# One pending tile's down projection placed behind the next tile's gate and up products, its transposes in another PSUM tensor

## The chip, the cores and the metric

The kernel runs on all 8 cores of one Trainium2 chip. Every core runs the same program on its own 2,048 tokens; the cores do not talk to each other. The metric is the device time of the slowest core, in microseconds (us).

## What is computed

One transformer layer on x of 4 x 4096 x 2048, in float32 outside the products: a retention-like attention block and a feed-forward block whose hidden values are made 2:4 sparse. The part that matters here is the second one:

```
x = x + layernorm(attn(layernorm(x)))
h = silu(xn @ w_gate) * (xn @ w_up)            # xn = layernorm(x); 2048 -> 8192
h = h where |h| is among the 2 largest of its group of 4, else 0
x = x + layernorm(h @ w_down)                  # 8192 -> 2048
```

## The kernel before

**Before the feed-forward block.** A core first runs the attention block over its 16 tiles of 128 tokens, up to about 2,480 us of the profile. It leaves the normalized and transposed tiles in DRAM (`s_xn3T`) and the residual in `s_x2`. Nothing of this is touched.

**The feed-forward block, `ffn()`** (lines 638 to 789). The 8192 hidden columns are cut into NIC = 8 blocks `ic` of ICW = 1024. For each block the loop runs over the 16 tiles `t`. One iteration does this:

- SP loads the tile from `s_xn3T` into `bpool[t % 2]` (L718).
- PE makes gate and up: 64 matmuls of 128x512 into `psA` (L729, L732), gate in the first 1024 columns of `psA`, up in the others.
- ACT takes Silu of gate (L740); DVE multiplies it with up (L746) into one of three buffers of h (the trace names them t_mat, l_mat and fp; in the last block only the first two are used, since `fpool[2]` is needed elsewhere).
- ACT writes |h| (L751); seven small DVE operations find the second largest of each group of four (L761 to L777), one compares (L781), and one masks h (L784). This is called the mask chain below.

**The drain.** `drain(...)` makes the down projection of one tile whose h is ready: PE transposes h (8 float32 transposes, L675), ACT copies them back as bf16 (L680), PE runs 32 matmuls of 128x512 into `psB` (L689), DVE copies `psB` out (L697), and POOL adds the result to `s_acc` in DRAM by an accumulating DMA (L704; L700 in the first block). A list `pending` holds the tiles whose drain is still to come. It holds up to two tiles in blocks 0 to 6 and one in block 7.

**The end of a block.** While tile 15 is in gate and up, `load_q` loads and casts the next block's gate and up weights (32 half rows, DMAs on SP, casts on ACT at L617 and DVE at L613). Then the tiles still pending are drained back to back, and `load_fdc` loads the down weights of the next block.

**The last block.** There each drain is followed by `emit_ln4`: SP reads the sum back from `s_acc` (L646), DVE and ACT compute the layer norm (L310, L313, L315, L318, L652), DVE adds the residual (L656), and SP stores the tile of y (L660).

**Order.** Each engine runs its own list of operations in the order in which `P.op` was called, SP's DMAs too. Before an operation, its engine waits for the semaphores of what it reads and overwrites, and nothing behind it starts until it has. `r_A[0]` and `r_A[1]` stand for the two halves of `psA`, `r_B[0]` and `r_B[1]` for those of `psB`. Below, d(t) is the drain of tile t and g(t) its gate and up matmuls.

Of the kernel before, what the change touches and what calls it, by code (L numbers as in the profile page):

```python
# [18 lines left out]
ICW = 1024  # L19
NIC = I // ICW  # L20
# [121 lines left out]
def build():  # L142
# [56 lines left out]
    psA = psm("psA", [128, D], F32)  # L199
    psB = psm("psB", [128, D], F32)  # L200
# [12 lines left out]
    P = Prog()  # L213
# [15 lines left out]
    r_ident = Res()  # L229
    r_vst = Res()  # L230
    r_carry = Res()
    r_A = [Res(), Res()]
    r_B = [Res(), Res()]
# [404 lines left out]
    def ffn():  # L638
# [6 lines left out]
        def emit_ln4(t):  # L645
            P.op("sync", lambda s, t=t: s.dma_start(out=fpool[2][:], in_=s_acc[t]),  # L646
                 dma=True, reads=[r_sacc[t]], writes=[r_fp[2]])
            mvp, rsp, rs = ln_stats(fpool[2][:], r_fp[2], par=t % 2)
            fx = t % 2
            P.op("sync", lambda s, t=t, fx=fx: s.dma_start(out=fpool[fx][:], in_=s_x2[t]),  # L650
                 dma=True, reads=[r_sx2[t]], writes=[r_fp[fx]])
            P.op("vector", lambda v, fx=fx, mvp=mvp, rsp=rsp: v.tensor_scalar(  # L652
                fpool[2][:], fpool[2][:], mvp[:, 0:1], rsp[:],
                ALU.subtract, ALU.mult),
                 reads=[rs], writes=[r_fp[2]])
            P.op("vector", lambda v, fx=fx: v.tensor_tensor(fpool[2][:], fpool[2][:],  # L656
                                                            fpool[fx][:], ALU.add),
                 reads=[r_fp[fx]], writes=[r_fp[2], r_fp[fx]])
            yres = Res()
            tok = P.op("sync", lambda s, t=t: s.dma_start(  # L660
                out=y_d[t * 128:(t + 1) * 128, :], in_=fpool[2][:]),
                dma=True, reads=[r_fp[2]], writes=[yres])
            out_toks.append(tok)

        def drain(pend):
            pt, pic = pend
            par = ((pic * NT + pt) % 3) if pic < NIC - 1 else (pt % 2)
            hsp = hbuf[par]
            hflat = hflats[par]
            rh = r_h[par]  # L670

            def trf(tt, hsp=hsp):
                ins = None
                for j in range(8):
                    ins = tt.transpose(psA[:, j * 128:(j + 1) * 128],  # L675
                                       hsp[:, j * 128:(j + 1) * 128], ident[:])
                return ins
            P.op("tensor", trf, reads=[rh, r_ident], writes=[r_A[0]])
            hT_flat = hflat
            P.op("scalar", lambda s, hT_flat=hT_flat: s.copy(hT_flat[:, 0:ICW],  # L680
                                                             psA[:, 0:ICW]),
                 reads=[r_A[0]], writes=[rh, r_A[0]])
            hT = hT_flat[:, 0:ICW].rearrange("p (a b) -> p a b", b=128)
            for q in range(4):
                def f(tt, q=q, hT=hT):
                    ins = None
                    for kc in range(q * 2, (q + 1) * 2):
                        for n in range(4):
                            ins = tt.matmul(psB[:, n * 512:(n + 1) * 512], hT[:, kc, :],  # L689
                                            fdc[:, kc, n * 512:(n + 1) * 512],  # L690
                                            start=(kc == 0), stop=(kc == ICW // 128 - 1))
                    return ins
                P.op("tensor", f, reads=[rh, r_fdc[q]], writes=[r_B[0], r_B[1]])
            dk = drr[0] % 4
            drr[0] += 1
            ev = stgF[dk]
            P.op("vector", lambda v, ev=ev: v.tensor_copy(ev[:], psB[:]),  # L697
                 reads=[r_B[0], r_B[1]], writes=[r_stgF[dk], r_B[0], r_B[1]])
            if pic == 0:
                P.op("gpsimd", lambda g, pt=pt, ev=ev: g.dma_start(  # L700
                    out=s_acc[pt], in_=ev[:]),
                    dma=True, reads=[r_stgF[dk]], writes=[r_sacc[pt]])
            else:
                P.op("gpsimd", lambda g, pt=pt, ev=ev: g.dma_start(  # L704
                    out=s_acc[pt], in_=ev[:], accum_op=ALU.add),
                    dma=True, reads=[r_stgF[dk]], writes=[r_sacc[pt]])
            if pic == NIC - 1:
                emit_ln4(pt)

        pending = []  # L710
        for ic in range(NIC):
            while pending:
                drain(pending.pop(0))
            load_fdc(ic)
            for t in range(NT):
# [2 lines left out]
                P.op("sync", lambda s, t=t, bx=bx: s.dma_start(out=bpool[bx][:],  # L718
                                                               in_=s_xn3T[t]),
                     dma=True, reads=[r_sxn3T[t]], writes=[r_bp[bx]])  # L720
                if len(pending) >= (2 if ic < NIC - 1 else 1):
                    drain(pending.pop(0))
                xT = bpool[bx][:].rearrange("p (a b) -> p a b", b=128)
                for q in range(4):
                    def f(tt, xT=xT, q=q):
                        ins = None
                        for kc in range(q * 4, (q + 1) * 4):
# [9 lines left out]
                         writes=[r_A[0], r_A[1]])  # L737
                    if t == NT - 1 and ic + 1 < NIC:
# [3 lines left out]
                     reads=[r_A[0]], writes=[r_fp[fx], r_A[0]])  # L742
# [6 lines left out]
                     reads=[r_A[1], r_fp[fx]], writes=[rht, r_A[1], r_fp[fx]])  # L749
# [3 lines left out]
                     reads=[rht], writes=[r_bp[2]])  # L753
# [9 lines left out]
                     reads=[r_bp[2]], writes=[r_bp[3]])  # L763
                P.op("vector", lambda v: v.tensor_tensor(mx1, a4[:, :, 0:1], a4[:, :, 1:2],  # L764
                                                         ALU.max),
                     reads=[r_bp[2]], writes=[r_bp[3]])
                P.op("vector", lambda v: v.tensor_tensor(mn2, a4[:, :, 2:3], a4[:, :, 3:4],
                                                         ALU.min),
                     reads=[r_bp[2]], writes=[r_bp[3]])
                P.op("vector", lambda v: v.tensor_tensor(mx2, a4[:, :, 2:3], a4[:, :, 3:4],  # L770
                                                         ALU.max),
                     reads=[r_bp[2]], writes=[r_bp[3]])
                P.op("vector", lambda v: v.tensor_tensor(mn1, mn1, mn2, ALU.max),
                     reads=[r_bp[3]], writes=[r_bp[3]])
                P.op("vector", lambda v: v.tensor_tensor(mx1, mx1, mx2, ALU.min),
                     reads=[r_bp[3]], writes=[r_bp[3]])
                P.op("vector", lambda v: v.tensor_tensor(mn1, mn1, mx1, ALU.min),  # L777
                     reads=[r_bp[3]], writes=[r_bp[3]])
# [4 lines left out]
                    reads=[r_bp[2]], writes=[r_bp[3]])  # L783
                P.op("vector", lambda v, cmpm=cmpm, hsl=hsl: v.tensor_tensor(  # L784
                    hsl[:, 0:ICW], hsl[:, 0:ICW], cmpm, ALU.mult),
                     reads=[r_bp[3]], writes=[rht])
                pending.append((t, ic))
        while pending:
            drain(pending.pop(0))
# [13 lines left out]
    handoff([r_fdc[0], r_fdc[1], r_fdc[2], r_fdc[3]] + r_stgF, r_wB)  # L803
    handoff([r_p0b[0], r_p0b[1]], [r_decay])
    ffn()
    P.barrier_wait("sync", out_toks)

# [49 lines left out]
```

How the kernel before makes its waits and increments, by code:

```python
            def body(h, ops=ops):  # L116
                for waits, fn, sname, n in ops:
                    for s, v in waits:
                        h.wait_ge(sems[s], v)
                    if fn is not None:
                        ins = fn(h)
                        if sname is not None:
                            ins.then_inc(sems[sname], n)
```

## Time and profile before

| | us |
|---|---|
| median of two runs | 6968.84 (6835.03 and 7102.64) |
| the profiled execution, its own time | 6868.66 |
| its span (slowest core, core 5) | 6867.1 |
| spans of the eight cores | 6807.3 to 6867.1 |
| PE busy in matmuls | 4399.4 (64%) |
| DVE busy | 2059.3 (30%) |
| ACT busy | 1007.7 (15%) |

The span runs from the first to the last instruction of a core. PE is TensorE, DVE is VectorE, ACT is ScalarE, POOL is GpSimd; SPq is the queue that issues most DMAs. Busy time of PE is made up of overlapping matmuls, so a 128x512 matmul shows as 0.38 us although one starts every 0.22 us. "PEclk" is the clock granted to TensorE as a share of 2.4 GHz. The feed-forward block takes about 4,380 of the 6,867 us: seven blocks of some 520 us and a last one of about 760.

### The profile page before, as it was taken

To read this page: it belongs to the slowest core of one execution; us is meant where nothing else is said; L and a number is where in the kernel's file an instruction comes from. 1 tells how busy PE (TensorE), PEld (TensorE's weight loads), DVE (VectorE), ACT (ScalarE), POOL (GpSimd) and SP (SyncE) were. 2 spreads that over 40 slices of the span, in tenths; PEclk is the share of its full clock that TensorE was granted. 3 is DMA by queue.
4 is the path that set the end of the run, shared out by engine and by line. 5 is a ranking of instruction groups with operands and counts; after the bars stand their busy time and mean duration, and the time that the engine had idled before them with its cause. 6 is when DMAs were issued, how large, how long until landed. Compare 5 with 4: busy or idle time off the path is not lost.

```text
span 6867.1 us, 51810 instructions; the slowest of 8 cores (6807.3 to 6867.1 us)
## 1 busy us (share of the span) xinstructions
PE 4399.4 (64%) x19374; PEld 2041.2 (30%) x19374; DVE 2059.3 (30%) x2796; ACT 1007.7 (15%) x1035; POOL 165.7 (2%) x232
## 2 busy tenths in 40 slices
PE   0236888547616668858758758858858848835554
PEld 0013444224303323323323323323323323312222
DVE  1523233212214433323223223322322323322333
ACT  2301111111111011111111111111111111111111
POOL 0000000000000000000000000000000000000000
PEclk9998778778858889979979979979979979967777
DMA  5400100132263331242352352352352352353333
GB/s 156 137 13 22 37 31 34 48 114 75 89 202 118 121 107 59 93 143 59 94 142 59 94 142 59 85 148 59 84 149 62 78 155 57 75 175 97 99 108 104
DMA packets 140830, 649.31 MB, mean 95 GB/s; under 512 B 15652, under 2 KB 15652, under 8 KB 107812
## 3 DMA queue, kind: packets, MB, share of 16 engines
q1 hardware_dynamic: 110630, 461.44, 20.6%
q0 software_dynamic: 29952, 184.56, 12.1%
q8 instruction: 156, 2.56, 0.2%
q14 instruction: 92, 0.75, 0.0%
HBM read 453.00 MB, written 192.94 MB: 94 GB/s over the span
## 4 chain that ended last, share of the span: by engine, by line
PE 57%; DMA 19%; DVE 10%; ACT 7%; issue 5%; SPq 1%; DVEq 0%; ACTq 0%; POOL 0%; POOLq 0%
PE psB L689 16%; PE psA L729 11%; PE psA L732 11%; PE psB L356 9%; PE psA L356 5%; DMA stg<-w_gate 3%; DMA stg<-w_down 2%; PE psA L336 2%; DMA stg<-w_up 2%; DMA s_acc<-wslotB 2%; ACT bp L751 2%; ACT fp L740 2%; DVE stats L310 1%; DMA stg<-Wg 1%; DMA stg<-Wo 1%
## 5 line engine op out<-in xcount | busy, mean ns | idle before, releaser
L729 PE MATMUL psA<-wslotA,bp 128*128 128x512 bf16 x4096 | 1566.8, 383 | 284.6 <-DMA bp<-s_xn3T 263.5
L732 PE MATMUL psA<-wslotA,bp 128*128 128x512 bf16 x4096 | 1565.8, 382 | 0.0
L729 PEld LDWEIGHTS psA<-wslotA,bp 128*128 128x128 bf16 x4096 | 403.6, 99 | 782.4 <-issue 307.9
L732 PEld LDWEIGHTS psA<-wslotA,bp 128*128 128x128 bf16 x4096 | 403.4, 98 | 490.0 <-issue 14.9
L356 PE MATMUL psB<-wslotA,bp 128*128 128x512 bf16 x2048 | 492.4, 406 | 44.2 <-ACT bp L341 44.2
L356 PE MATMUL psA<-wslotB,bp 128*128 128x512 bf16 x1536 | 373.3, 409 | 207.6 <-DMA bp<-s_ygT 207.6
L697 DVE COPY wslotB<-psB 128x2048 f32<-128x2048 f32 x128 | 293.3, 2291 | 673.4 <-PE psB L689 673.4
L740 ACT ACTIVATE fp<-psA 128x1024 f32<-128x1024 f32 x128 | 131.0, 1024 | 2310.9 <-PE psA L732 2310.8
L689 PE MATMUL psB<-wslotB,t_mat 128*128 128x512 bf16 x1472 | 397.0, 437 | 96.9 <-DVE bp L764 74.5
L689 PE MATMUL psB<-wslotB,l_mat 128*128 128x512 bf16 x1440 | 393.6, 441 | 95.0 <-DVE bp L764 76.6
L689 PE MATMUL psB<-wslotB,fp 128*128 128x512 bf16 x1184 | 319.3, 437 | 84.0 <-DVE bp L764 73.6
L336 PE MATMUL psA<-ident,fp 128*128 128x128 f32 x768 | 144.5, 368 | 267.0 <-DVE fp L519 216.5
L356 PEld LDWEIGHTS psB<-wslotA,bp 128*128 128x128 bf16 x2048 | 208.9, 103 | 322.0 <-issue 147.9
L356 PEld LDWEIGHTS psA<-wslotB,bp 128*128 128x128 bf16 x1536 | 158.6, 104 | 417.8 <-issue 298.7
L613 DVE CAST wslotA<-stg 128x1024 bf16<-128x1024 f32 x160 | 111.0, 694 | 547.6 <-DMA stg<-w_up 349.1
L689 PEld LDWEIGHTS psB<-wslotB,t_mat 128*128 128x128 bf16 x1472 | 157.9, 109 | 325.9 <-issue 205.6
L689 PEld LDWEIGHTS psB<-wslotB,l_mat 128*128 128x128 bf16 x1440 | 155.4, 110 | 323.3 <-issue 207.8
L617 ACT CAST wslotA<-stg 128x1024 bf16<-128x1024 f32 x160 | 167.0, 1044 | 560.6 <-DMA stg<-w_gate 312.9
L675 PE MATMUL psA<-ident,l_mat 128*128 128x128 f32 x360 | 56.6, 309 | 297.3 <-DVE l_mat L784 159.4
L675 PE MATMUL psA<-ident,t_mat 128*128 128x128 f32 x368 | 57.6, 308 | 284.0 <-DVE t_mat L784 146.6
L310 DVE BATCH_NORM_STATS2 stats<-fp 128x6 f32<-128x512 f32 x256 | 158.0, 679 | 234.3 <-DMA fp<-s_acc 224.6
L336 PEld LDWEIGHTS psA<-ident,fp 128*128 128x128 f32 x768 | 133.1, 197 | 282.8 <-issue 279.8
(128 smaller groups left out, 3250.0 us busy)
## 6 DMA issues: line engine op xcount, KB each, us to landing
s_acc<-wslotB POOLq DMA_DIRECT2D x128, 1024.0 KB, 7.7
stg<-w_gate SPq DMA_DIRECT2D x128, 512.0 KB, 5.6
stg<-w_up SPq DMA_DIRECT2D x128, 512.0 KB, 5.9
stg<-w_down SPq DMA_DIRECT2D x128, 512.0 KB, 6.1
bp<-s_xn3T SPq DMA_DIRECT2D x128, 512.0 KB, 3.3
fp<-x SPq DMA_DIRECT2D x48, 1024.0 KB, 5.2
stg<-Wq SPq DMA_DIRECT2D x32, 512.0 KB, 4.8
stg<-Wv SPq DMA_DIRECT2D x32, 512.0 KB, 4.5
```

Of the source, the lines that this page charges most:

```text
L310: ins = v.bn_stats(st6[:, 6 * i:6 * i + 6], src_ap[:, 512 * i:512 * (i + 1)])
L336: ins = t.transpose(psA[:, half * 1024 + j * 128:half * 1024 + (j + 1) * 128], src_ap[:, kc * 128:(kc + 1) * 128], ident[:])
L356: ins = t.matmul(psum[:, n * 512:(n + 1) * 512], xT_ap[:, kc, :], w_sb[:, kc, n * 512:(n + 1) * 512], start=(kc == 0), stop=(kc == KC - 1))
L613: P.op("vector", lambda v, dst_ap=dst_ap, k=k: v.tensor_copy(dst_ap, wstg4[k]), reads=[r_wstg4[k]], writes=[dst_res, r_wstg4[k]])
L617: P.op("scalar", lambda s, dst_ap=dst_ap, k=k: s.copy(dst_ap, wstg4[k]), reads=[r_wstg4[k]], writes=[dst_res, r_wstg4[k]])
L675: ins = tt.transpose(psA[:, j * 128:(j + 1) * 128], hsp[:, j * 128:(j + 1) * 128], ident[:])
L689: ins = tt.matmul(psB[:, n * 512:(n + 1) * 512], hT[:, kc, :], fdc[:, kc, n * 512:(n + 1) * 512], start=(kc == 0), stop=(kc == ICW // 128 ...
L697: P.op("vector", lambda v, ev=ev: v.tensor_copy(ev[:], psB[:]), reads=[r_B[0], r_B[1]], writes=[r_stgF[dk], r_B[0], r_B[1]])
L729: ins = tt.matmul(psA[:, n * 512:(n + 1) * 512], xT[:, kc, :], fgc[:, kc, n * 512:(n + 1) * 512], start=(kc == 0), stop=(kc == KC - 1))
L732: ins = tt.matmul(psA[:, 1024 + n * 512:1024 + (n + 1) * 512], xT[:, kc, :], fuc[:, kc, n * 512:(n + 1) * 512], start=(kc == 0), stop=(kc ...
L740: P.op("scalar", lambda s, fx=fx: s.activation(fpool[fx][:, 0:ICW], psA[:, 0:ICW], AF.Silu), reads=[r_A[0]], writes=[r_fp[fx], r_A[0]])
L751: P.op("scalar", lambda s, hsl=hsl: s.activation(habs[:, 0:ICW], hsl[:, 0:ICW], AF.Abs), reads=[rht], writes=[r_bp[2]])
```

## The change

Two things change in `ffn()`, and no amount of work changes. The transposes of h go to `psB` instead of `psA`, and the ACT copy reads them from there. The call of `drain` inside the tile loop moves from ahead of the gate and up matmuls of tile t to behind the mask chain of tile t; the number of tiles that may be pending stays two, or one in the last block.

```diff
@@ drain
-                    ins = tt.transpose(psA[:, j * 128:(j + 1) * 128],
+                    ins = tt.transpose(psB[:, j * 128:(j + 1) * 128],
                                        hsp[:, j * 128:(j + 1) * 128], ident[:])
-            P.op("tensor", trf, reads=[rh, r_ident], writes=[r_A[0]])
+            P.op("tensor", trf, reads=[rh, r_ident], writes=[r_B[0]])
             P.op("scalar", lambda s, hT_flat=hT_flat: s.copy(hT_flat[:, 0:ICW],
-                                                             psA[:, 0:ICW]),
-                 reads=[r_A[0]], writes=[rh, r_A[0]])
+                                                             psB[:, 0:ICW]),
+                 reads=[r_B[0]], writes=[rh, r_B[0]])
@@ tile loop of ffn
                 P.op("sync", lambda s, t=t, bx=bx: s.dma_start(out=bpool[bx][:],
                                                                in_=s_xn3T[t]),
                      dma=True, reads=[r_sxn3T[t]], writes=[r_bp[bx]])
-                if len(pending) >= (2 if ic < NIC - 1 else 1):
-                    drain(pending.pop(0))
                 xT = bpool[bx][:].rearrange("p (a b) -> p a b", b=128)
...
                      reads=[r_bp[3]], writes=[rht])
+                maxp = 2 if ic < NIC - 1 else 1
+                if len(pending) >= maxp:
+                    drain(pending.pop(0))
                 pending.append((t, ic))
```

## Rows read from the trace of the kernel before

**Rows 1.** Timeline of one tile in block 2: start us, us, engine, line, idle before.

```profile
3714.53 1.02 ACT L740 ACTIVATE fp<-psA 128x1024 f32<-128x1024 f32 x1 [22.84 <-PE psA L732]
3715.73 1.22 DVE L746 TENSOR_TENSOR t_mat<-psA,fp 128x1024 f32<-128x1024 f32 x1 [12.64 <-ACT fp L740]
3715.81 1.06 PE L675 MATMUL psA<-ident,fp 128*128 128x128 f32 x8 [1.38 <-ACT fp L740]
3717.05 1.06 ACT L751 ACTIVATE bp<-t_mat 128x1024 bf16<-128x1024 f32 x1 [1.49 <-DVE t_mat L746]
3718.01 0.99 ACT L680 CAST fp<-psA 128x1024 bf16<-128x1024 f32 x1
3719.25 8.68 PE L689 MATMUL psB<-wslotB,fp 128*128 128x512 bf16 x32 [2.38 <-DVE bp L764]
3728.10 2.29 DVE L697 COPY wslotB<-psB 128x2048 f32<-128x2048 f32 x1 [3.97 <-PE psB L689]
```

**Rows 2.** Timeline of ACT in block 1: Silu of two successive tiles.

```profile
3362.96 1.02 ACT L740 ACTIVATE fp<-psA 128x1024 f32<-128x1024 f32 x1 [22.84 <-PE psA L732]
3390.26 1.02 ACT L740 ACTIVATE fp<-psA 128x1024 f32<-128x1024 f32 x1 [22.84 <-PE psA L732]
```

**Rows 3.** The same view, tiles 0 and 1 of block 2, with no drain between.

```profile
3533.79 1.02 ACT L740 ACTIVATE fp<-psA 128x1024 f32<-128x1024 f32 x1 [17.04 <-PE psA L732]
3550.91 1.02 ACT L740 ACTIVATE fp<-psA 128x1024 f32<-128x1024 f32 x1 [13.20 <-PE psA L732]
```

**Rows 4.** Busy time by stretch, two parts of one down projection; PEclk is the clock.

```profile
core 5: us, PE busy (x) PEld busy (x) DVE busy (x) ACT busy (x) POOL busy (x), PEclk, DMA share, GB/s
3719.20:3722.50 3.30, 3.25 (x8) 1.20 (x9) 2.68 (x7) 0.00 (x0) 0.00 (x0) 0.50 0.00 0
3722.70:3727.50 4.80, 4.80 (x24) 2.16 (x22) 1.33 (x2) 0.00 (x0) 0.00 (x0) 1.00 0.00 0
```

**Rows 5.** Timeline around the change from block 6 to block 7.

```profile
6057.12 8.80 PE L689 MATMUL psB<-wslotB,fp 128*128 128x512 bf16 x32 [1.43 <-DVE bp L764]
6066.10 2.29 DVE L697 COPY wslotB<-psB 128x2048 f32<-128x2048 f32 x1 [4.17 <-PE psB L689]
6068.54 7.07 PE L689 MATMUL psB<-wslotB,t_mat 128*128 128x512 bf16 x32 [1.74 <-DVE wslotB L697]
6075.78 2.29 DVE L697 COPY wslotB<-psB 128x2048 f32<-128x2048 f32 x1 [7.39 <-PE psB L689]
6110.21 0.59 PE L729 MATMUL psA<-wslotA,bp 128*128 128x512 bf16 x1 [34.61 <-DMA bp<-s_xn3T]
6126.77 1.02 ACT L740 ACTIVATE fp<-psA 128x1024 f32<-128x1024 f32 x1 [21.17 <-PE psA L732]
```

**Rows 6.** Timeline of block 7: parts of one cycle, the first and last eviction.

```profile
6398.40 2.47 DVE L310 BATCH_NORM_STATS2 stats<-fp 128x6 f32<-128x512 f32 x4 [13.39 <-DMA fp<-s_acc]
6402.93 1.28 ACT L740 ACT_TABLE_LOAD   x1
6407.01 1.22 DVE L746 TENSOR_TENSOR t_mat<-psA,fp 128x1024 f32<-128x1024 f32 x1
6407.76 0.32 SPq L718 DMA_DIRECT2D bp<-s_xn3T  x1
6415.49 1.94 PE L675 MATMUL psA<-ident,t_mat 128*128 128x128 f32 x8 [19.13 <-DVE t_mat L784]
...
6148.39 2.29 DVE L697 COPY wslotB<-psB 128x2048 f32<-128x2048 f32 x1 [12.01 <-PE psB L689]
6837.41 2.29 DVE L697 COPY wslotB<-psB 128x2048 f32<-128x2048 f32 x1 [12.47 <-PE psB L689]
```

**Rows 7.** Waits in block 7: total us, times, longest us.

```profile
DVE stats L310 <- DMA fp<-s_acc: 210.2, 15, 17.3
```

**Rows 8.** Landing of the loads from s_xn3T: in block 7, then in blocks 1 and 2.

```profile
DMA to landing us min/median/max: 5.4/5.4/5.5
DMA to landing us min/median/max: 3.1/3.3/8.3
```

## The prediction

> **What bounds the kernel now.** I read the busy table by stretch first, then the timeline of one tile in a middle block, then the ends of a block, and last the timeline, the waits and the chain of block 7, where the order of a tile's work is another.
>
> In blocks 0 to 6 TensorE sets the pace, with one pause per tile. [rows 1] show it: gate and up end at about 3714.4, and the down matmuls start at 3719.25. Read what lies between on the ACT queue: Silu at 3714.53, |h| at 3717.05, which had to wait for DVE's product at 3715.73, and the copy of the transposed h of the tile two back at 3718.01, right behind |h|. The transposes ended at 3716.87. So the copy was held 1.1 us by ACT's order, not by TensorE. The DVE name beside the down matmuls is only an operation that ended at the time. A tile takes 27.30 us from Silu to Silu [rows 2]; without a drain between, 17.12 us [rows 3].
>
> After the pause the clock is at half level: 0.50 for the first 3.3 us of the down matmuls, which is 1.2 GHz, then 1.00 [rows 4]. The 32 matmuls take 8.68 us, against 7.07 us where it did not fall [rows 1, 5].
>
> In block 7 another loop sets the pace. The drain of t-1 comes ahead of gate and up of t, but needs the mask chain of t-1, and this sits on DVE behind the layer norm of t-2, which waits for its sum to go to DRAM and back. TensorE stands 19.13 us before the transposes [rows 6]. The 16 evictions run from 6148.39 to 6837.41, so a cycle is 689.02/15 = 45.93 us.
>
> **Part 1: transposes in `psB`, drain behind the mask chain, blocks 0 to 6.** TensorE may now start the transposes right after gate and up, without waiting for Silu. But the copy's place on ACT is the same as before: Silu, |h|, copy. In the new order it is again the third of the three, and |h| still needs the product on DVE. From Silu to the start of the down matmuls stays 3719.25 - 3714.53 = 4.72 us. `psB` is free by then: its eviction from the tile before ends some 13 us earlier (2.29 us of DVE just after the down matmuls [rows 1]). What the transposes win, about 1.4 us, is spent waiting for the copy. I cost it at nothing; the cover is the ACT queue. The bounds are the clock's (rivals 2 and 4).
>
> **Part 2: the ends of the blocks, seven times.** Before, 14 drains lie in a block's loop and two behind the weight load; now 13 and three. In the loop one interval of 27.30 becomes 17.12: -10.18 us. Behind the load, before: down(14) starts at 6057.12 and the eviction of down(15) at 6075.78, so 18.66 us [rows 5]. After: three drains in a row, and the transposes of the second and third must wait until `psB` is evicted, where in `psA` they ran beside it. The first: eviction 8.98 us after its start, 2.29 for it, about 0.15 to hand over, 1.06 transposes, 0.13, copy 1.01, 0.25 = 13.87 us to the next start. The second has 8.85 or 7.24 us to its eviction, as the clock falls [rows 1] or not [rows 5], plus the same 4.89; the third only 8.85 or 7.24. Sum 36.46 or 33.24, less 18.66: +17.80 or +14.58. Net +7.62 or +4.40 a block end, 53 or 31 us in all. I take the middle, +42.
>
> **Part 3: block 7, where SP's order decides.** The drain carries `emit_ln4`, and with it four DMAs' worth of SP order: read of the sum, residual, store of y, and behind them, in the next iteration, the load of the next tile from `s_xn3T`. Before, the load of tile t+1 was behind the store of y(t-1) too, but gate and up of t and the long drain of t lay between; it was issued at 6407.76 and needed a drain later. Now gate and up of t+1 is the very next thing on TensorE behind down(t-1), and its input is queued on SP behind the store of y(t-1), which waits for layer norm(t-1), which waits for down(t-1). What used to be two overlapping tiles becomes one serial chain. Queued behind the late load: gate and up, Silu, product, mask chain and the next drain. Its length, from eviction to eviction:
>
> - eviction 2.29 + DVE's wait for the sum to come back, 210.2/15 = 14.01 [rows 7]: 16.30
> - statistics to the issue of the load, 6398.40 to 6407.76 [rows 6]: 9.36
> - the load's landing, behind the y store: 5.4 [rows 8]
> - gate and up after a long idle stretch, 6110.21 to 6126.77 [rows 5]: 16.56
> - table load before Silu 1.28 [rows 6]; so far it ran while DVE did the norm, now behind the wait for gate and up
> - Silu to down 4.72, down to eviction 3728.10 - 3719.25 = 8.85 [rows 1]
>
> Sum 62.47 us, 16.54 more than 45.93. It runs 14 times (from drain 0 to drain 14): +231.6. At its start, eviction 0 comes at 6126.77 + 17.12 + 4.72 + 8.85 = 6157.46 in place of 6148.39: +9.07. At its end, drain 15 needs no load: its copy waits on ACT for the square root of tile 14, 16.30 + (6402.93 - 6398.40) = 20.83, then 1.01 + 0.14 + 8.85 makes 30.83 in place of 45.93: -15.10. Block 7: +226.
>
> The wait for the mask chain (19.13 us) does go away in this block, as the move suggests; but the load that takes its place is later by more.
>
> **Sum.** 0 + 42 + 226 = +268 us on the profiled execution's 6868.66: 7137 us, 3.9% more. The runs shown of before stand 34 us below and 234 above that execution, so the profiled one is near the lower of them, and against their median of 6968.84 the forecast is 2.4% more.
>
> Bounds of block 7: the landing 3.1 to 5.5 (-32, +1); no table load in the way (-18); the return of the sum, longest wait 17.3 in place of 14.01 (+46); gate and up at full clock, twice the 7.07 us of 32 matmuls = 14.1 in place of 16.56 (-34, though after 30 us idle I expect the row). With the block ends, +-11, the forecast's own range is 7050 to 7200.
>
> On the table load the Trainium skill ("ScalarE: Activation LUTs", What ACT_TABLE_LOAD costs) gives some 1.38 us of drain beside each load of 1.28; the trace shows none, since the load starts at 6402.93, as the square root ends. By the page the cycle would be 1.38 longer and the sum 19 us higher; I go by the row.
>
> **Rivals.**
>
> 1. *Not slower: the load of the next tile is early enough.* If it were issued before down(t-1) ends, gate and up would follow at once and DVE's loop would be the limit: 16.30, statistics to product 6407.01 - 6398.40 = 8.61, product to down 3.52, 8.85 = 37.28 us a cycle. 15 x (37.28 - 45.93) + 9 = -121, with the block ends 6790 us (-1.1%). For it: 19 us of waiting is really there. Against: L660 and L718 are both on SP, in order. Chance 0.05.
> 2. *The clock stops falling in blocks 0 to 6.* 8.85 - 7.24 = 1.61 us for each of 13 x 7 = 91 drains: -147, 6990 us (+1.8%). Against it: the transposes now close up to gate and up, and what follows is one unbroken stop of about 3.6 us instead of two of 1.38 and 2.38. The Trainium skill ("TensorE: Matmul & The Clock Gate", HAM oscillation) says that pauses between bursts throttle the clock anew at each burst; one longer pause is no better by that. Chance 0.07.
> 3. *The copy comes sooner*: if only transposes and copy stood between gate and up and down, the pause would be some 2.4 us shorter, 91 x 2.4 = -218, 6919 us (+0.7%). ACT's order is against it. Chance 0.03.
> 4. *The clock falls for longer* because of the unbroken stop: twice the loss, +147, 7284 us. Chance 0.05.
>
> **How the numbers follow.** The forecast has 0.78, the rivals 0.20, and 0.02 is for what I don't see. A measurement can tell about 2% from no change. Slower by over 2%: the forecast and rival 4, 0.84. Within 2%: rivals 1 to 3 nearly whole, 0.13. Faster: 0.03. The range takes the forecast's own, the 34 us by which another run of before was lower, and part of rival 4 and of the spread upward: 7040 to 7250.
>
> **What would show it.** Silu to Silu stays at 27.3 us in a middle block, with the transposes starting right behind gate and up. Three down projections stand behind each weight load, 12 to 14 us apart. In block 7 the evictions are about 62 us apart, TensorE's wait before L729 is for the DMA of `s_xn3T` (some 30 us, 14 times), the wait for L784 is gone, and the granted clock there is no higher. It is wrong if L729 in block 7 starts right behind L689, or if the middle blocks' interval moves by more than 0.3 us.

## The result, and the profile after

| | before | after |
|---|---|---|
| median of all executions, us | 7037.06 (10) | 7134.37 (11) |
| profiled execution, us | 6868.66 | 7097.72 |
| span of its slowest core, us | 6867.1 | 7096.2 |
| ratio, 95% interval | | 1.0401 (1.0368 to 1.0434) |

The change makes the kernel 4.0% slower. In some executions the cores of one die, or of both, show a lower granted clock and take some per cent longer; the ratios and the execution times below leave those out, and only the two medians hold them, which is why they lie closer together.

The busy table of the page of the changed kernel, and its largest matmul group, with the same group of the kernel before as the last line (line, engine, operation, shapes, count | busy, mean ns | idle before it and what ended most of that):

```profile
span 7096.2 us, 51582 instructions; the slowest of 8 cores (7059.8 to 7096.2 us)
PE 4367.4 (62%) x19374; PEld 2031.5 (29%) x19374; DVE 2061.2 (29%) x2796; ACT 1002.6 (14%) x1033; POOL 165.1 (2%) x232
L727 PE MATMUL psA<-wslotA,bp 128*128 128x512 bf16 x4096 | 1585.8, 387 | 742.9 <-DMA bp<-s_xn3T 699.8
L729 PE MATMUL psA<-wslotA,bp 128*128 128x512 bf16 x4096 | 1566.8, 383 | 284.6 <-DMA bp<-s_xn3T 263.5
```

The work is what it was; L727 (L729 before) now waits 699.8 us for loads from `s_xn3T`, where it waited 263.5.

A middle tile of the changed kernel, in the timelines of ACT and PE (start us, us, engine, line, idle before), which answers to [rows 1]:

```profile
3702.03 1.02 ACT L738 ACTIVATE fp<-psA 128x1024 f32<-128x1024 f32 x1 [22.81 <-PE psA L730]
3704.55 1.06 ACT L749 ACTIVATE bp<-l_mat 128x1024 bf16<-128x1024 f32 x1 [1.49 <-DVE l_mat L744]
3705.51 0.99 ACT L680 CAST fp<-psB 128x1024 bf16<-128x1024 f32 x1
3701.77 1.04 PE L675 MATMUL psB<-ident,fp 128*128 128x128 f32 x8
3706.64 8.75 PE L689 MATMUL psB<-wslotB,fp 128*128 128x512 bf16 x32 [3.84 <-ACT fp L680]
```

The transposes start 0.26 us before Silu, where they were 1.28 us behind it; the copy is still third on ACT. From Silu to the down matmuls it takes 4.61 us (4.72 before), and the 84 intervals between evictions in the loops average 27.28 us (91 of 27.33 before).

The end of block 6, PE timeline, which answers to [rows 5]. Only the second and third of the three drains are shown:

```profile
6060.15 1.06 PE L675 MATMUL psB<-ident,fp 128*128 128x128 f32 x8 [2.61 <-DVE wslotB L697]
6062.46 8.75 PE L689 MATMUL psB<-wslotB,fp 128*128 128x512 bf16 x32 [1.25 <-ACT fp L680]
6073.83 1.06 PE L675 MATMUL psB<-ident,t_mat 128*128 128x128 f32 x8 [2.61 <-DVE wslotB L697]
6076.20 8.75 PE L689 MATMUL psB<-wslotB,t_mat 128*128 128x512 bf16 x32 [1.30 <-ACT t_mat L680]
```

Both transposes wait 2.61 us for DVE to empty `psB`. The starts are 13.74 us apart, against 11.42 us of the two before.

One cycle of block 7, DVE, SP, PE and ACT timelines, which answers to [rows 6]:

```profile
6416.85 2.29 DVE L697 COPY wslotB<-psB 128x2048 f32<-128x2048 f32 x1 [3.62 <-PE psB L689]
6432.73 2.47 DVE L310 BATCH_NORM_STATS2 stats<-fp 128x6 f32<-128x512 f32 x4 [13.58 <-DMA fp<-s_acc]
6441.89 0.34 SPq L660 DMA_DIRECT2D y<-fp  x1
6442.44 0.32 SPq L718 DMA_DIRECT2D bp<-s_xn3T  x1
6448.09 0.59 PE L727 MATMUL psA<-wslotA,bp 128*128 128x512 bf16 x1 [31.41 <-DMA bp<-s_xn3T]
6464.09 1.28 ACT L738 ACT_TABLE_LOAD   x1 [26.86 <-PE psA L730]
6465.38 1.02 ACT L738 ACTIVATE fp<-psA 128x1024 f32<-128x1024 f32 x1
6470.00 9.93 PE L689 MATMUL psB<-wslotB,l_mat 128*128 128x512 bf16 x32 [5.17 <-ACT l_mat L680]
6480.10 2.29 DVE L697 COPY wslotB<-psB 128x2048 f32<-128x2048 f32 x1 [5.18 <-PE psB L689]
```

Read it downward: eviction, sum through DRAM, layer norm, store of y, and only then, 0.55 us behind the store on the same queue, the load that TensorE has been waiting for. The table load stands behind the wait for gate and up, not under it. The waits view of block 7 sums it up (total us, times, longest):

```profile
PE psA L727 <- DMA bp<-s_xn3T: 406.2, 13, 32.9
```

That is 31.2 us each, for the 13 of the 14 tiles that the stretch holds. The wait of the transposes for the mask chain (19.13 us in [rows 6]) is gone.

### The profile page after: what moved, and what is told of

Read it like the earlier page. It is cut to its first block, busy times and chain, and to the rows that moved or that the text cites. A ratio compares the mean times of both kernels' runs of the same rounds, so it can differ in the third digit from the quotient of the medians.

```text
span 7096.2 us, 51582 instructions; the slowest of 8 cores (7059.8 to 7096.2 us)
## 1 busy us (share of the span) xinstructions
PE 4367.4 (62%) x19374; PEld 2031.5 (29%) x19374; DVE 2061.2 (29%) x2796; ACT 1002.6 (14%) x1033; POOL 165.1 (2%) x232
## 4 chain that ended last, share of the span: by engine, by line
PE 58%; DMA 19%; DVE 8%; ACT 8%; issue 6%; SPq 1%; DVEq 0%; ACTq 0%; POOL 0%; POOLq 0%
PE psB L689 16%; PE psA L727 12%; PE psA L730 12%; PE psB L356 8%; PE psA L356 5%; DMA stg<-w_gate 4%; PE psA L336 2%; DMA stg<-w_down 2%; DMA bp<-s_xn3T 2%; ACT fp L738 2%; DMA s_acc<-wslotB 2%; DMA stg<-w_up 1%; DVE stats L310 1%; DMA stg<-Wv 1%; DMA stg<-Wo 1%
## 5 line engine op out<-in xcount | busy, mean ns | idle before, releaser
L727 PE MATMUL psA<-wslotA,bp 128*128 128x512 bf16 x4096 | 1585.8, 387 | 742.9 <-DMA bp<-s_xn3T 699.8
L730 PE MATMUL psA<-wslotA,bp 128*128 128x512 bf16 x4096 | 1583.7, 387 | 0.0
L727 PEld LDWEIGHTS psA<-wslotA,bp 128*128 128x128 bf16 x4096 | 407.4, 99 | 1260.7 <-issue 798.4
L689 PE MATMUL psB<-wslotB,t_mat 128*128 128x512 bf16 x1472 | 403.8, 443 | 263.5 <-ACT t_mat L680 263.5
L356 PE MATMUL psA<-wslotB,bp 128*128 128x512 bf16 x1536 | 352.0, 392 | 209.9 <-DMA bp<-s_ygT 209.9
L689 PEld LDWEIGHTS psB<-wslotB,fp 128*128 128x128 bf16 x1184 | 128.6, 111 | 408.3 <-issue 314.1
L744 DVE TENSOR_TENSOR t_mat<-psA,fp 128x1024 f32<-128x1024 f32 x46 | 56.3, 1225 | 638.6 <-ACT fp L738 638.3
L744 DVE TENSOR_TENSOR l_mat<-psA,fp 128x1024 f32<-128x1024 f32 x45 | 55.1, 1225 | 619.9 <-ACT fp L738 619.8
```

Of the source, the lines that this page charges most:

```text
L356: ins = t.matmul(psum[:, n * 512:(n + 1) * 512], xT_ap[:, kc, :], w_sb[:, kc, n * 512:(n + 1) * 512], start=(kc == 0), stop=(kc == KC - 1))
L727: ins = tt.matmul(psA[:, n * 512:(n + 1) * 512], xT[:, kc, :], fgc[:, kc, n * 512:(n + 1) * 512], start=(kc == 0), stop=(kc == KC - 1))
L730: ins = tt.matmul(psA[:, 1024 + n * 512:1024 + (n + 1) * 512], xT[:, kc, :], fuc[:, kc, n * 512:(n + 1) * 512], start=(kc == 0), stop=(kc ...
L744: P.op("vector", lambda v, fx=fx, hsl=hsl: v.tensor_tensor(hsl[:, 0:ICW], psA[:, ICW:2 * ICW], fpool[fx][:, 0:ICW], ALU.mult), reads=[r_A[ ...
```

## The experiments

All kernels compute the full result. Where a ratio has no interval, there were too few executions for one.

**Block 7 in the old order.** The changed kernel, except that in block 7 the drain stands ahead of gate and up again.

```diff
+                if ic == NIC - 1 and len(pending) >= 1:
+                    drain(pending.pop(0))
                 xT = bpool[bx][:].rearrange("p (a b) -> p a b", b=128)
...
-                maxp = 2 if ic < NIC - 1 else 1
-                if len(pending) >= maxp:
+                if ic < NIC - 1 and len(pending) >= 2:
                     drain(pending.pop(0))
```

> The changed kernel with one thing undone: in block 7 alone the drain stands ahead of gate and up again. Theory (block 7's serial chain through the load of the next tile is the loss, the block ends cost a little): evictions in block 7 are 46 us apart again, L729's wait for the DMA is gone, the block ends keep their three drains, so the kernel takes about 42 us more than before: ratio 1.006. Rival (the loss is spread over all blocks, by the later drain or by psB): ratio stays near 1.03 to 1.04.

Measured: 6877.09 us in one execution, beside 6836 to 6857 us of before in the same job: about 1.005, near the 1.006 expected. The evictions of block 7 are 45.7 us apart on average (686.2/15). So block 7 holds nearly all of the loss, and the rival is out; what is left has the size of the block ends' term.

**Only the load moved.** The changed kernel, but in block 7 SP issues the load of tile t+1 ahead of the drain.

```diff
+                if ic < NIC - 1 or t == 0:
+                    load_x(t)
...
+                if ic == NIC - 1 and t + 1 < NT:
+                    load_x(t + 1)
                 maxp = 2 if ic < NIC - 1 else 1
                 if len(pending) >= maxp:
                     drain(pending.pop(0))
```

> The changed kernel, with one DMA moved: in block 7 the load of tile t+1 is issued on SP ahead of the drain, so ahead of the store of y. Theory (SP's order makes the chain serial): gate and up follow down at once, and DVE's loop sets the cycle: 37.3 us between evictions in place of 62.5, so ratio about 0.989 to before. Rival (the chain is serial for another reason, such as psB or the layer norm on DVE itself): cycles stay at 55 us or more, ratio 1.02 or more.

Measured: ratio 0.9964 (0.9941 to 0.9986). One DMA's place on SP takes back more than the whole loss. But 14 cycles average 40.7 us, not 37.3. The ACT timeline of this kernel shows what was left out:

```profile
6435.20 1.28 ACT L315 ACT_TABLE_LOAD   x1 [29.02 <-DVE mv L313]
6436.50 0.29 ACT L315 ACTIVATE sd<-mv,c_eps 128x1 f32<-128x1 f32 x1
6441.05 1.28 ACT L741 ACT_TABLE_LOAD   x1 [4.26 <-DVE fp L656]
6442.35 1.02 ACT L741 ACTIVATE fp<-psA 128x1024 f32<-128x1024 f32 x1
```

Silu waited 4.26 us for L656, the addition of the residual. The residual of tile t-1 is loaded into `fpool[(t-1) % 2]`, and that is the buffer into which Silu of t+1 writes.

**The residual apart.** The same kernel, with the residual in block 7 in `stg`, which no weight needs any more there.

```diff
-            P.op("sync", lambda s, t=t, fx=fx: s.dma_start(out=fpool[fx][:], in_=s_x2[t]),
-                 dma=True, reads=[r_sx2[t]], writes=[r_fp[fx]])
+            P.op("sync", lambda s, t=t, fx=fx: s.dma_start(out=stg[fx][:], in_=s_x2[t]),
+                 dma=True, reads=[r_sx2[t]], writes=[r_wstg4[2 * fx], r_wstg4[2 * fx + 1]])
```

> The kernel with the early load in block 7, and there the residual goes to the idle staging buffers in place of the buffer that Silu of tile t+1 also writes. Theory (in the run with the early load, Silu waited 4.3 us for the residual's addition, since both use the same buffer, and that is the gap between 40.7 and the worked-out 37.3 us): cycles of 37.3 us, ratio 0.989. Rival (the sum's way through DRAM is what grew): cycles stay at 40 us or more.

Measured: ratio 0.9882 (0.9854 to 0.9910); 14 cycles average 37.7 us. The shared buffer was the missing 3 us. This is the first rival of the prediction (37.28 us a cycle, 1.1% less than before), measured: it comes true once two conditions hold, not one.

**Only `psB`.** The kernel before, its transposes in `psB`, the drain in its old place.

> The kernel before with the transposes in psB and the drain in its old place. Theory: the copy is third on ACT either way, so a middle tile stays at 27.3 us; at each block end the second of two drains waits for the eviction of psB, some 2.4 us more, 17 us in all, ratio 1.002. Rival (transposes free of Silu shorten the pause): middle tiles at 24.9 to 26 us, ratio 0.97 to 0.98.

Measured: ratio 1.0031 (1.0015 to 1.0047). The middle intervals average 27.28 us. At the block ends the second drain's eviction comes 13.6 to 14.7 us after the first's, where it was 9.68 before: 4 to 5 us more, not 2.4.

**Only the order.** The kernel before, the drain in its new place, the transposes in `psA`.

> The kernel before with the drain in its new place and the transposes still in psA. Theory: middle tiles stay at 27.3 us, since transposes wait for Silu but the copy waits for |h| anyway; block ends cost about 1 us each in place of 6, block 7 costs what it does in the changed kernel, 226 us. Ratio 1.034. Rival (psB is what costs): ratio under 1.01.

Measured on cores 0 to 3 of its profiled execution: spans of 7042.8 to 7054.7 us, beside 6775 to 6856 us for the single cores of before in the same job, about 1.03. On core 0 fourteen cycles of block 7 average 63.2 us, the middle intervals 27.33, and the evictions of the three drains at the ends are 9.68 us apart (13.5 to 14.7 in the changed kernel). So the order carries the loss, and `psB` adds a small one at the ends.

**The copy first.** The changed kernel with `drain` cut in two; transposes and ACT copy of the pending tile now come right behind Silu, the rest stays behind the mask chain.

```diff
+                maxp = 2 if ic < NIC - 1 else 1
+                late = pending.pop(0) if len(pending) >= maxp else None
+                if late is not None:
+                    drain_head(late)
                 hpar = ((ic * NT + t) % 3) if ic < NIC - 1 else (t % 2)
...
-                maxp = 2 if ic < NIC - 1 else 1
-                if len(pending) >= maxp:
-                    drain(pending.pop(0))
+                if late is not None:
+                    drain_tail(late)
```

> The changed kernel with one order changed: the transposes and the ACT copy of the pending tile come right behind Silu, ahead of the product and of |h|. Theory (in the middle blocks the copy's third place on ACT holds the down matmuls): the pause loses |h| and the wait for the product, some 2.5 us, so evictions stand about 24.8 us apart in place of 27.28 if the clock falls as it did, 23.2 if it falls no more; 84 intervals, 206 us or more less than the changed kernel. Block 7's cycle falls from 62 to about 59.5 too. Ratio to before 1.005. Rival (the interval of 27.3, the same in both kernels to 0.05 us, is set by something else, such as the clock's own rhythm): it stays at 27.3, or moves by under 1 us.

Measured: 6643.86 us in one execution, beside 6837 to 6859 us of before: 0.970. The middle intervals average 23.05 us, and fourteen cycles of block 7 58.6 us (59.5 expected). The expected ratio of 1.005 was worked out for a clock that still falls. Its timelines and clock (the last row: stretch, busy us with counts, PEclk 1.00):

```profile
3702.48 1.01 ACT L680 CAST fp<-psB 128x1024 bf16<-128x1024 f32 x1
3704.07 1.06 ACT L762 ACTIVATE bp<-l_mat 128x1024 bf16<-128x1024 f32 x1 [0.59 <-DVE l_mat L757]
3703.63 7.07 PE L694 MATMUL psB<-wslotB,fp 128*128 128x512 bf16 x32 [1.29 <-ACT fp L680]
3703.50:3710.50 7.00, 6.87 (x32) 3.16 (x33) 4.85 (x10) 1.06 (x1) 0.00 (x0) 1.00 0.01 2
```

The stop after the transposes is 1.29 us in place of 3.84, and the down matmuls take 7.07 us in place of 8.75: 2.55 and 1.68 add up to the 4.23 us by which each of the 84 intervals is shorter. The order on ACT was the bound, and with a stop of 1.29 us the clock stays at its upper level, 2.4 GHz, in the middle tiles.

**The copy first, in `psA`.** The same with the transposes back in `psA`.

> The run with the copy first on ACT, but with the transposes back in psA, where they wait for Silu. Theory (psB is worth something only once the copy is no longer behind |h|): the pause grows by about 1.1 us from 1.3 + 1.0, to some 3.4 us; the interval of the middle blocks is 24.2 us if the clock stays at its upper level, 25.8 if it falls again. Rival (psB is worth nothing): 23.05 us as in that run.

Measured: 6846 and 6856 us, beside 6644 us of the run above (of another job) and 6839 us of before. So `psB` is worth about 200 us once the copy is first. Before that it cost: 1.0031 alone, and 1.040 in place of about 1.03 in the new order. Two successive tiles in the PE timeline of core 4:

```profile
3800.23 1.06 PE L675 MATMUL psA<-ident,fp 128*128 128x128 f32 x8 [1.26 <-ACT fp L747]
3802.65 7.07 PE L694 MATMUL psB<-wslotB,fp 128*128 128x512 bf16 x32 [1.36 <-ACT fp L680]
3824.80 1.06 PE L675 MATMUL psA<-ident,t_mat 128*128 128x128 f32 x8 [1.26 <-ACT fp L747]
3827.22 8.74 PE L694 MATMUL psB<-wslotB,t_mat 128*128 128x512 bf16 x32 [1.36 <-ACT t_mat L680]
```

The transposes wait 1.26 us for Silu, then the matmuls 1.36 us for the copy. With the same two stops the clock stays up in the first tile and falls in the second. On this core Silu to Silu takes about 24.57 us where it stays up and 26.25 where it falls (24.2 and 25.8 expected), and it falls in 28 of 84.

**How long a stop the clock bears.** The copy first, with one or two idle ACT copies of 1.04 us ahead of the copy of h.

```diff
+                P.op("scalar", lambda s, fx=fx: s.copy(vst[:, 0:ICW], fpool[fx][:, 0:ICW]),
+                     reads=[r_fp[fx]], writes=[r_vst])
                 maxp = 2 if ic < NIC - 1 else 1
```

> The run with the copy first, with one idle copy of 128x1024 (1.0 us) laid on ACT between Silu and the copy of h, in every tile; its result is not used. The unbroken stop of TensorE grows from 1.3 to about 2.3 us. If the clock still doesn't fall, the middle interval is 24.05 us; if it does, about 25.7.

> The same with two idle copies of 1.0 us each, whose result is not used: a stop of about 3.3 us. 25.05 us if the clock doesn't fall, 26.7 if it falls as in the changed kernel. Together with the run before: a jump of more than 1.0 us between neighbours shows at which stop the clock's loss sets in.

Measured: middle intervals of 24.49 us on average with one filler and 26.73 with two, the same on all eight cores to 0.01 us. One line with one filler (core 4), then two successive ones with two (core 2), PE timeline:

```profile
3124.58 7.07 PE L694 MATMUL psB<-wslotB,l_mat 128*128 128x512 bf16 x32 [2.44 <-ACT l_mat L680]
...
3118.42 7.07 PE L694 MATMUL psB<-wslotB,fp 128*128 128x512 bf16 x32 [3.56 <-ACT fp L680]
3143.74 8.75 PE L694 MATMUL psB<-wslotB,t_mat 128*128 128x512 bf16 x32 [3.57 <-ACT t_mat L680]
```

A tile whose clock stays up has 24.18 us with one filler (Silu at 3121.37 and 3145.55) and 25.32 with two (3114.07 and 3139.39). Above that the means lie 0.3 and 1.4 us; a full fall costs 1.68. Counted, the clock falls in 15 of 84 intervals on core 4 with one filler, and in 70 of 84 on core 2 with two. So at 2.44 us of stop a fall is the exception, at 3.57 us the rule.

**The chain broken.** The copy first, the early load, and in block 7 the layer norm of a tile one tile later, so that DVE does not wait for the sum.

```diff
             if pic == NIC - 1:
-                emit_ln4(pt)
+                lnq.append(pt)
+                if len(lnq) > 1:
+                    emit_ln4(lnq.pop(0))
```

> Copy first, the early load in block 7, and there the layer norm of a tile comes one tile later, so that DVE no longer waits for the sum to come back. Theory: block 7 becomes a TensorE loop like the others, 13.8 + Silu, table load and copy + down = 26 to 28 us a cycle in place of 62; with the middle blocks at 24.8 us, some 6410 us in all, ratio 0.935. If the middle interval stays at 27.3: 6600 us, 0.96.

Measured: ratio 0.9006 (0.8981 to 0.9032), 6167 us. The cycles of block 7 are 23.1 to 25.9 us. It is faster than expected, because the clock stays up in the middle blocks: (24.8 - 23.05) x 84 = 147 us of the 243. Fifteen cycles of block 7 at 24.2 us, where 26 to 28 were expected, give some 40 more; for the rest I have no account.

**The block ends filled.** Also the weights' casts laid between the drains and the first tiles, and each tile's load issued a tile ahead.

```diff
+                if lastt:
+                    load_q(ic + 1, 1)
+                    drain(pending.pop(0))
+                    load_q(ic + 1, 2)
+                    drain(pending.pop(0))
+                    load_x(0)
+                    load_q(ic + 1, 3)
+                if ic > 0 and t < 2 and ic < NIC - 1:
+                    load_fdc_half(ic, t)
+                if ic == NIC - 1 and t == 0:
+                    load_fdc(ic)
```

> The kernel before this one, and at each block end the weights' casts are laid between the drains, the down weights' casts between the first tiles, and each tile's load is issued one tile ahead. Theory: of the 75 us that a block end spends on loading with TensorE idle, some 50 to 70 us go under other work, seven times: 350 to 480 us less than the kernel before this one, ratio about 0.87 to 0.89. Rival (the memory is the bound at the ends): under 100 us.

Measured: 5852 and 5860 us, beside 6837 to 6859 us of before: 0.855. Against the version before it that is about 310 us less, under the 350 expected. In the profiled executions TensorE's idle time between the Silu of tile 14 and that of the next block's tile 0 falls from 88 to 38 us. Some of that is given back in block 7, where the first eviction comes 44.1 us behind the first Silu in place of 26.3, with the load of the down weights now between them. The casts and the earlier loads were changed together, so what each is worth is not shown.

> The version with the copy first, the early load, the late layer norm and the interleaved weight loads, taken again for an interval of its ratio: 0.855, from its profiled execution of 5857.9 us span against 6836 to 6869 us of before.

Measured: 5855, 5870 and 5889 us, beside 6839 us: 0.858. This version takes 14 to 15% less than the kernel before, which is itself 4% below the changed one.

## Why the prediction came out as it did

The forecast was 7137 us, +268 us or 3.9% on the profiled execution. The median after is 7134 us, and the ratio 1.040. That the two times meet is partly luck: the base of 6868.66 us lies some 27 us above other short executions of before (6835 to 6842 us), and the median after holds long executions too. Step by step:

- **Middle blocks, 0 us.** 27.33 became 27.28 us. Right, and for the reason given: the copy stayed third on ACT [rows 1], and moving it ahead, with the transposes, gave 4.23 us a tile.
- **Block ends, +42 us.** From the Silu of tile 0 in block 0 (2503.82 and 2458.33) to that in block 7 (6126.77 and 6133.09) are seven blocks: 517.56 us each before, 524.97 after. +7.4 us each, +52 in all, on the slowest core of each execution: near the upper bound given (7.6), since the clock falls in each of the later drains (8.75 us, not 7.07). I took the middle of the two, and on these cores the term is 10 us too small. The drains themselves confirm the upper figure: from the first of these down projections to the last eviction the mean over all eight cores is 18.96 us before and 36.89 after, +17.9 (17.80 worked out). But whole blocks, with their weight loads, average 518.8 us before and 523.8 after over the eight cores, and 524.2 to 525.5 in three of the experiments with the same block ends: +35 to +47 us in all. The term is known to no better than that.
- **Block 7, cycle.** Worked out 62.47 us; the 14 cycles average 62.48. That close it is partly luck: on the seven other cores they average 61.5 to 62.2 us, and in the cycle shown the way from the statistics to the load took 9.71 (9.36 taken), the landing 5.65 (5.4), gate and up 16.00 (16.56), the table load 1.28 (1.28), Silu to down 4.62 (4.72) and down to eviction 10.10 (8.85), and the sum's return 15.88 (16.30).
- **Block 7, ends.** Eviction 0 came 30.29 us after Silu of tile 0 (30.69), the last interval is 30.14 us (30.83).
- **The sum.** The feed-forward block grew by 52 for seven blocks, 9 for its first eviction, and 904.8 - 689.0 = 216 in block 7, together 277 us. The two profiled spans differ by only 229, because the part before the feed-forward block, which the change does not touch, was 45 us shorter on the core shown after (2458.33 us to the first Silu, 2503.82 before). The same stretch of that part in both executions, the kernel before first:

```profile
580.00:870.00 290.00, 247.79 (x1055) 117.55 (x1054) 79.63 (x100) 44.49 (x39) 2.85 (x5) 0.76 0.09 34
580.00:870.00 290.00, 242.11 (x1181) 121.68 (x1180) 97.19 (x123) 50.78 (x45) 3.38 (x6) 0.89 0.11 40
```

The granted clock of core 5 is 0.76 there, 0.89 on the core after, and fewer matmuls are done. The ratio over many executions shows the full 4.0%.

**The step that failed** is in the prediction's sum: the sentence that set the forecast beside the median of the two runs shown, and the range in microseconds that was built on the same absolute times. 7137 over 6968.84 gave "2.4% more", and the ratio is 4.0%. The two runs (6835.03 and 7102.64) lie 268 us apart, as far as the whole forecast change, so their median was no base; the working's own, 6868.66 us, was the one to compare with. With ten executions the median of before came to 7037, which makes the same 7137 us only 1.4%, while 1.040 times that median is 7319 us, above the range of 7040 to 7250. I should have stated one expected ratio, 1.039, and taken the range and the chance of "slower" from it alone. The waits and the paths that the prediction named are the ones that the runs show; of its terms the block ends were the one furthest off, at +42 for the 52 us of the cores above.

**The rivals.** Rival 1 gave 37.28 us a cycle if the load were early. With the load early it was 40.7: the working missed that Silu of t+1 and the residual of t-1 share a buffer, a wait that lay under the late load. With that wait gone too it is 37.7. Rival 3 gave 2.4 us for a copy that comes sooner. In the change it does not come sooner; once the order on ACT is changed, the stop shrinks by 2.55 us, but the clock's 1.68 us comes on top. The two were priced as separate rivals and go together. Rivals 2 and 4, the clock rising or falling further with the unbroken stop, did not come about in the change: 8.75 us of down against 8.68.

On the table load before Silu, the trace after shows 1.28 us followed at once by Silu (6464.09 and 6465.38). The 1.38 us of drain that the Trainium skill gives beside it ("ScalarE: Activation LUTs", What ACT_TABLE_LOAD costs) shows nowhere here, so the row was the better guide.

## What to carry to other kernels

When a piece of work is moved on one engine, walk its whole issue order on the others: here the gain was looked for on TensorE, the bound sat in ACT's order, and the loss came from a load that stood behind a store on SP. Take the waits away one after the other, since each hides the next (load, then buffer, then the sum's return), and issue the next tile's load ahead of anything in its queue that waits for the tile before. To shorten a stop of TensorE can be worth more than its length, where it decides whether the clock falls. And set a forecast beside a base of its own kind, a ratio beside a ratio.

## What the runs showed of the hardware that was not expected

The clock's loss comes with small differences of the stop before the down matmuls. In the middle tiles, after 64 dense matmuls (about 14 us) and the transposes, an unbroken stop of 1.29 us left the granted clock at 1.00 and down at 7.07 us. A stop of 2.44 us cost something in 15 of 84 tiles, 3.57 us in 70 of 84, and 3.84 us took the clock to 1.2 GHz each time (8.75 us).

But the unbroken stop alone does not decide. In the kernel before, two stops of 1.38 and 2.38 us, with 1.06 us of transposes between them, cost the same 1.6 us at each tile [rows 1], although neither is longer than 2.44. At the ends of the changed kernel stops of 2.61 and 1.25 us around the transposes go with 8.75 us too. And with `psA` and the copy first, the same two stops of 1.26 and 1.36 us left the clock up in one tile and took it down in the next. What else decides was not tried further.
